# Four conditioned layers on one core: softmax probabilities normalised by POOL before the transposes, instead of the attention outputs by VectorE after the values product

## What is computed

```python
# layer 0: 16 heads of 32, 4 key/value heads, causal in blocks of 128
h = layernorm(x) * (1 + scale) + shift
q, k = rope(h @ Wq.T), rope((h @ Wkd.T) @ Wku.T);  v = (h @ Wkd.T) @ Wvu.T
x = x + softmax(q @ k.T / sqrt(32) + mask) @ v @ Wo.T
# layer 1: 8 heads of 64, one key/value head, then a gated MLP of 2048
q, k, v = rope(h @ Wq.T), rope(h @ Wk.T), h @ Wv.T
x = x + softmax(q @ k.T / 8) @ v @ Wo.T
x = x + (silu(h2 @ Wg.T) * (h2 @ Wu.T)) @ Wd.T
# layer 2: 16 heads of 32, q and k of unit length, bias, then a gelu MLP of 2048
x = x + gamma1 * (softmax(qn @ kn.T + bias) @ v @ Wproj.T + bproj)
x = x + gamma2 * (gelu(h2 @ Wfc1.T) @ Wfc2.T)
# layer 3: experts, layernorm, silu, projection
```

## Times and profile before

| | us |
|---|---|
| runs of the kernel before (3) | 2496.61, 2500.17, 2505.05; median 2500.17 |
| profiled execution | 2504.14, its span 2502.1 |
| PE, PEld busy | 2361.6 (94%), 1477.7 (59%) |
| DVE, ACT, POOL busy | 1199.7 (48%), 1062.8 (42%), 267.2 (11%) |
| attention of layer 0, 1, 2 in the span | 91 to 476, 476 to 843, 1437 to 2005 |

### The profile page before, as it was taken

How to read it: one execution, slowest core, us unless ns; L and a number is a source line. 1 busy time by engine, 2 the same in 40 slices (tenths; PEclk the granted TensorE clock), 3 DMA queues, 4 the chain that set the end, 5 groups by cost and what they waited for, 6 DMA issues and landing times.

```text
span 2502.1 us, 32257 instructions
## 1 busy us (share of the span) xinstructions
PE 2361.6 (94%) x13000; PEld 1477.7 (59%) x13000; DVE 1199.7 (48%) x2466; ACT 1062.8 (42%) x2407; POOL 267.2 (11%) x222
## 2 busy tenths in 40 slices
PE   6889999999999999999999989999999889999998
PEld 2445555455555687888877544445455568888633
DVE  2465564553446434333443254638367655444332
ACT  2465565543435321111113155638457652222373
POOL 3332021121121000000000010101001110000021
PEclk8899999999999999999999979999999999999999
DMA  9200010000001000000001000000001011000001
GB/s 311 72 17 17 1 34 10 9 5 5 9 10 42 26 1 26 26 26 26 26 7 67 17 1 1 1 1 1 1 1 35 18 51 34 17 17 1 1 18 51
DMA packets 45236, 64.95 MB, mean 26 GB/s; under 512 B 8368, under 2 KB 21952, under 8 KB 45088
## 3 DMA queue, kind: packets, MB, share of 16 engines
q1 hardware_dynamic: 44112, 60.38, 7.5%
q0 software_dynamic: 976, 2.51, 0.3%
HBM read 52.66 MB, written 4.19 MB: 23 GB/s over the span
## 4 chain that ended last, share of the span: by engine, by line
PE 85%; ACT 6%; DVE 6%; issue 1%; POOL 1%; DMA 0%; SPq 0%; POOLq 0%; ACTq 0%; DVEq 0%
PE banks L1026 35%; PE banks L388 22%; PE banks L663 8%; PE banks L655 6%; PE banks L679 5%; DVE sb_Pr L735 2%; ACT sb_Pr L765 2%; PE banks L486 1%; PE banks L261 1%; PE banks L689 1%; PE banks L426 1%; ACT sb_PT L770 1%; PE banks L561 1%; PE banks L569 1%; DVE sb_hN L352 1%; ACT sb_t L299 1%
## 5 line engine op out<-in xcount | busy, mean ns | idle before, releaser
L1026 PE MATMUL banks<-sb_HH,sb_Ws 128*128 128x512 f32 x1536 | 494.8, 396 | 12.7 <-DVE sb_HL L943 7.2
L663 PEld LDWEIGHTS banks<-sb_ident,sb_Pr 128*128 128x128 f32 x2176 | 242.7, 143 | 213.8 <-issue 82.2
L663 PE MATMUL banks<-sb_ident,sb_Pr 128*128 128x128 f32 x2176 | 316.7, 284 | 34.7 <-DVE sb_PT L742 12.1
L1026 PEld LDWEIGHTS banks<-sb_HH,sb_Ws 128*128 128x128 f32 x1536 | 291.9, 190 | 78.4 <-issue 17.6
L1026 PE MATMUL banks<-sb_hidH,sb_Ws 128*128 128x512 f32 x1024 | 332.1, 394 | 0.0
L765 ACT ACTIVATE sb_Pr<-sb_Pr,sb_nmax 128x512 f32<-128x512 f32 (+3 forms) x512 | 321.7, 635 | 22.1 <-DVE sb_nmax L735 22.1
L735 DVE CUSTOM_DVE_ANT_0 sb_Pr<-banks,sb_bias 128x512 f32<-128x512 f32 (+3 forms) x512 | 273.7, 587 | 113.8 <-PE banks L655 108.7
L1026 PE MATMUL banks<-sb_HL,sb_Ws 128*128 128x512 f32 x768 | 301.7, 393 | 0.0
L770 ACT ACTIVATE sb_PT<-banks 128x512 f32<-128x512 f32 (+3 forms) x320 | 154.4, 528 | 326.0 <-PE banks L663 325.3
L388 PE MATMUL banks<-sb_hN,sb_W 128*128 128x512 f32 x576 | 268.3, 610 | 9.5 <-ACT sb_hN L321 6.4
L742 DVE COPY sb_PT<-banks 128x512 f32<-128x512 f32 (+3 forms) x320 | 181.1, 603 | 165.0 <-PE banks L663 164.4
(11 more groups left out here) (128 smaller groups left out, 2558.4 us busy)
## 6 DMA issues: line engine op xcount, KB each, us to landing
sb_staged<-in_L_cond_Wfc SPq DMA_DIRECT2D x16, 512.0 KB, 4.3
sb_wada<-in_L_cond_Wada SPq DMA_DIRECT2D x6, 1024.0 KB, 5.6
sb_x<-in_x SPq DMA_DIRECT2D x4, 1024.0 KB, 9.8
sb_staged<-in_L_cond_Wg SPq DMA_DIRECT2D x8, 512.0 KB, 3.5
sb_staged<-in_L_cond_Wu SPq DMA_DIRECT2D x8, 512.0 KB, 4.5
sb_staged<-in_L_cond_Wd SPq DMA_DIRECT2D x8, 512.0 KB, 3.6
out_x<-sb_x SPq DMA_DIRECT2D x4, 1024.0 KB, 4.5
sb_R<-sb_R SPq DMA_DIRECT2D x60, 64.0 KB, 2.0
```

Source lines behind the costliest of these rows:

```text
L663: mm = e.transpose(bank[:, j * P:(j + 1) * P], k.Pr[:, n % 6, j * P:(j + 1) * P], k.ident[:])
L1026: mm = e.matmul(bank, lhsT, rhs, start=i == 0, stop=i == len(mats) - 1)
```

## The change

The probabilities of each unit are normalised before they are transposed. DVE takes the reciprocals of two units' sums at a time (`recip`, 320 instead of 48 instructions, 2 columns instead of 16 or 8), POOL multiplies each unit's probabilities in place by its reciprocal, a column that is repeated along the row (`divide`, 640 instructions on POOL, as wide as the unit's scores), and `turn` waits for `divide` instead of `exp`. The spreads (PE) and the divisions of the outputs (DVE) are gone; the output projection waits for `out`. In the sequence the reciprocal of units 2 and 3 of quad t stands ahead of the four maxima of quad t+1, and that of units 0 and 1 of quad t+1 stands behind its last exponentials and ahead of the copies of units 2 and 3 of quad t. POOL's multiplications follow each.

```diff
@@ Heads.pe
         elif kind == "turn":
-            for due in after(s.name, b, "exp", u):
+            for due in after(s.name, b, "divide", u):
                 e.wait_ge(*due)
@@
-        else:
-            for due in after(s.name, b, "recip", u):
-                e.wait_ge(*due)
-            bank = s.tab.claim(e, s, b, kind, u, after)
-            for i in range(TT):
-                for hl in range(s.per):
-                    o = s.column(u, i, hl)
-                    mm = e.matmul(bank[hl * s.dv:(hl + 1) * s.dv, i * P:(i + 1) * P],
-                                  k.rsum[:, b % 2, o:o + 1].to_broadcast([P, s.dv]), k.ident[:], start=True, stop=True)
@@ Heads.dve
-        elif kind == "recip":
-            for due in after(s.name, b, "exp", (u + 1) * 2 * s.G - 1):
-                e.wait_ge(*due)
-            o = slice(s.column(u, 0, 0), s.column(u + 1, 0, 0))
+        else:
+            for due in after(s.name, b, "exp", 2 * u + 1):
+                e.wait_ge(*due)
+            c, _, i, hl = s.units[2 * u]
+            o = slice(s.column(c, i, hl), s.column(c, i, hl) + 2)
             ins = e.reciprocal(k.rsum[:, b % 2, o], k.sums[:, b % 2, o])
-        else:
-            for due in after(s.name, b, "out", u):
-                e.wait_ge(*due)
-            for due in after(s.name, b, "spread", u):
-                e.wait_ge(*due)
-            ins = e.tensor_tensor(s.out(b, u), s.out(b, u), s.tab.at[(s.name, b, "spread", u)], ALU.mult)
         ins.then_inc(k.done["dve"], 1)
+
+    def pool(s, k, e, b, kind, u, after):
+        for due in after(s.name, b, "recip", u // 2):
+            e.wait_ge(*due)
+        prob = k.Pr[:, (s.first[b] + u) % 6, 0:s.width(u)]
+        e.tensor_tensor(prob, prob, s.stat(k, k.rsum, b, u).to_broadcast([P, s.width(u)]), ALU.mult)\
+            .then_inc(k.done["pool"], 1)
@@ weave
+    def recip(t, half):
+        for h, b, u in units(t)[2 * half:2 * half + 1]:
+            seq.append((h, b, "dve", "recip", u // 2))
+            seq.extend([(h, b, "pool", "divide", u), (h, b, "pool", "divide", u + 1)])
+
...
         copy(t, 0)
         copy(t, 1)
+        recip(t, 1)
         for i in range(4):
             soft(t + 1, i, "dve", "max")
         soft(t + 1, 0, "act", "exp")
         soft(t + 1, 1, "act", "exp")
         point(m)
-        for h, b, c in spreads:
-            seq.extend([(h, b, "pe", "spread", c), (h, b, "dve", "divide", c)])
-        spreads = []
...
                 if g % 2:
-                    seq.extend([(h, b, "act", "out", g // 2), (h, b, "dve", "recip", g // 2)])
-                    spreads.append((h, b, g // 2))
+                    seq.append((h, b, "act", "out", g // 2))
         point(m)
         turn(t, 2)
         turn(t, 3)
         soft(t + 1, 2, "act", "exp")
         soft(t + 1, 3, "act", "exp")
+        recip(t + 1, 0)
         copy(t, 2)
         copy(t, 3)
@@ conditioned_stack
-        divided = lambda name, b: (lambda c: [(name, b, "divide", c)])
+        valued = lambda name, b: (lambda c: [(name, b, "out", c)])
```

More of the change, by code:

```diff
@@ L663, in pe @@
                 mm = e.transpose(bank[:, j * P:(j + 1) * P], k.Pr[:, n % 6, j * P:(j + 1) * P], k.ident[:])
-        elif kind == "values":
+        else:
             c, ip = divmod(u, 2)
@@ L681, in pe @@
                                   start=j == 0, stop=j == tiles - 1)
-        else:
-            for due in after(s.name, b, "recip", u):
-                e.wait_ge(*due)
-            bank = s.tab.claim(e, s, b, kind, u, after)
-            for i in range(TT):
-                for hl in range(s.per):
-                    o = s.column(u, i, hl)
-                    mm = e.matmul(bank[hl * s.dv:(hl + 1) * s.dv, i * P:(i + 1) * P],
-                                  k.rsum[:, b % 2, o:o + 1].to_broadcast([P, s.dv]), k.ident[:], start=True, stop=True)
         mm.then_inc(k.done["pe"], 1)
     def reader(s, kind, u):
-        return {"scores": (s.released, u), "turn": ("copy", u), "spread": ("divide", u), "values": ("out", u // 2)}[kind]
+        return {"scores": (s.released, u), "turn": ("copy", u), "values": ("out", u // 2)}[kind]
     def copy_waits(s, e, k, b, u, after):
@@ L742, in dve @@
             ins = e.tensor_copy(*s.turned(k, b, u))
-        elif kind == "recip":
-            for due in after(s.name, b, "exp", (u + 1) * 2 * s.G - 1):
+        else:
+            for due in after(s.name, b, "exp", 2 * u + 1):
                 e.wait_ge(*due)
-            o = slice(s.column(u, 0, 0), s.column(u + 1, 0, 0))
+            c, _, i, hl = s.units[2 * u]
+            o = slice(s.column(c, i, hl), s.column(c, i, hl) + 2)
             ins = e.reciprocal(k.rsum[:, b % 2, o], k.sums[:, b % 2, o])
-        else:
-            for due in after(s.name, b, "out", u):
-                e.wait_ge(*due)
-            for due in after(s.name, b, "spread", u):
-                e.wait_ge(*due)
-            ins = e.tensor_tensor(s.out(b, u), s.out(b, u), s.tab.at[(s.name, b, "spread", u)], ALU.mult)
-        ins.then_inc(k.done["dve"], 1)
+        ins.then_inc(k.done["dve"], 1)
+    def pool(s, k, e, b, kind, u, after):
[4 more added lines that the diff above has]
+            .then_inc(k.done["pool"], 1)
     def act(s, k, e, b, kind, u, after):
@@ L910, in weave @@
         point(m)
-    assert not spreads and seen[len(mains)] >= len(closing)
+    assert seen[len(mains)] >= len(closing)
     return seq
@@ L1329, in conditioned_stack @@
         scaled = lambda name, b: (lambda c: [(name, b, "scale", c)])
-        divided = lambda name, b: (lambda c: [(name, b, "divide", c)])
+        valued = lambda name, b: (lambda c: [(name, b, "out", c)])
         def post(n, w, gamma=None, free=None, load=None):
             return SideLinear(f"post{n}", [
-                Group(lambda b, g=g: product(w, g, lambda c: attended(b, c), divided(f"heads{n}", b)), "dve",
+                Group(lambda b, g=g: product(w, g, lambda c: attended(b, c), valued(f"heads{n}", b)), "dve",
                       residual_put(g, gamma), load=load, free=free and (lambda b, g=g: free(b, g))) for g in range(C)])
```

## The result

The changed kernel takes 2606.2 us (median of 4 runs, 2603.9 to 2619.2) against 2502.3 for the kernel before: a ratio of 1.043, 95% interval [1.039, 1.047]. Its profiled execution took 2604.7, with a span of 2602.6. It is slower, as forecast, by 104 us where 39 were expected, and it lies outside the range (2470 to 2600).

A forecast was written before the change was run, and what follows sets the result against it. TensorE's in-order queue was taken to bound the kernel. From 2504.1 us, 89 of lateness behind POOL less 50 for removed spreads gave 2543, less 4 to the median 2539; range 2470 to 2600.

The forecast's parts named there:

- What bounds it (TensorE's queue): All three attention stretches: TensorE sets the time, busy 2361.6 of 2502.1 us, with only some 78 us idle there.
- Removal, 50 us: TensorE's queue: 48 spreads take 47 us, up to 22 of waits go too; 50 of 47 to 69 taken.
- POOL's price, 1.23 us: POOL's 640 multiplications: 1.23 us for 512 columns, scaled with width, as its adds and products start 1.23 apart.
- case 3: POOL: repeated-column multiplication cheaper, 0.85 us for 512 columns; lateness 41, gain 67, 2474 us; meets gain at 0.92-1.06; chance 0.22.
- The reciprocals' size (0.15 us each): VectorE: 320 reciprocals of 2 columns at 0.15 us, 48 us in all, about equal to the 44 that leave.
- Their place: VectorE's queue: reciprocals wait for exponentials ahead of maxima, or stand behind side work; counting this, lateness is 143 us.
- case 2: VectorE's queue: the reciprocals' places count too, +143 - 50 = +93, so 2593 us; chance 0.21.
- Lateness, 89 us: TensorE waiting for POOL's queue: 89 us, 39 in layer 0, 9 in layer 1, 41 in layer 2.
- The ledger: All 320 pairs: POOL's possible end compared with TensorE's start, new lateness carried on; 89 us in sum.
- the sum itself, 2504.1 + 89 - 50: Whole kernel: profiled time plus POOL's lateness less the removal, 2543 us, less 4 to the median, 2539.
- Direction and chance (slower, 0.68): Whole kernel: slower by more than 7.5 us, chance 0.68; faster 0.22, within 0.10.
- The signs named: Profile: POOL rows near 1.23 us, POOL 65-75% busy in layer 0, TensorE idle for POOL over 60 us around batch ends.

The follow-up runs named there:

- no_norm: The changed kernel without its reciprocals and multiplications, transposes waiting for the exponentials (probabilities not normalised): 2474.4 us, ratio 0.989 to the kernel before.
- before: The kernel before the change, with spreads and divisions: 2502.3 us.
- the ladder: Kernels adding the change's parts in turn: removal 2474.4 us, reciprocals 2501.8, multiplication two columns wide 2531.6, half width 2557.6, full change 2606.2.
- recip_only: no_norm with the 320 small reciprocals kept at their places in VectorE's queue, nothing waiting for them: 2501.8 us, ratio 1.000 to the kernel before.
- recip_late: The changed kernel with the reciprocals of units 2 and 3 behind the next quad's four maxima: 2690.6 us, ratio 1.077 to the kernel before.
- pool_alone: The changed kernel without reciprocals, POOL multiplying at full width by the row's sum after the pair's exponentials: 2609.7 us, ratio 1.043 to the kernel before.
- after: The complete changed kernel: 2606.2 us, ratio 1.043 to the kernel before.

## Why the prediction was wrong, step by step

- **What bounds it (TensorE's queue).** Right: TensorE still carries 78% of the chain that ended last.
- **Removal, 50 us.** The work that left is 49.9 by the table (50.4 in no_norm), so the step of 16 and 8 products by 1.01 and 0.92 us holds. What it yields is less: no_norm is 25 us faster as a median, 29.6 in the profiled span. Its idle time is the same as before's (143.6 and 140.5), so the waits for the spreads' bank moved elsewhere, and it has 35 us more at 1.2 GHz. I gave their part (up to 22) almost no gain, rightly, but had no term for a loss.
- **POOL's price, 1.23 us.** Too high. Two multiplications behind each other at 512 columns take 2.04 us (the timeline row under the ladder), one 1.039 by the rows, so they start 1.00 apart; for 128, 256 and 384 columns it is 0.36, 0.57 and 0.78. POOL's adds and products of two full operands stay at 1.27 to 1.32. So a repeated column is cheaper. The Trainium skill (GPSIMD Engine Reference, Performance versus the Vector engine) gives about 2.6 cycles an element for a two-operand `tensor_tensor` and, for the best case of a loop, 1.8, 769 ns for 512 elements; the measured 1.00 us lies above the latter, and neither figure is for this form. 1.00 lies inside the 0.92 to 1.06 where case 3 was to meet the gain; the kernel is nevertheless 100 us slower, so the condition of case 3 was as good as met and its result was far off.
- **The reciprocals' size (0.15 us each).** Right: 159 ns, 51.0 us in all against 48. **Their place** was weighed as a case of its own (case 2) and left out of the sum. It belonged in: VectorE waits 105.3 us, in 114 pieces, for an exponential ahead of them, recip_only pays 27 us for them, and recip_late shows what a later start does.
- **Lateness, 89 us.** TensorE's idle time grew by 84.7, in the layers by 40.6, 7.7 and 35.4 against 39, 9 and 41. This agreement is in part luck. The ledger stood at 89 for a price of 1.23 and at 41 for 0.85, so in a straight line some 60 for 1.00 (an estimate), without the reciprocals' places; with them it stood at 143 for 1.23. The price was too high, a real wait was left out, and the two errors worked against each other; how nearly they cancelled is not shown.
- **The step that failed: the sum itself, 2504.1 + 89 - 50.** It priced a wait of TensorE at its length and left TensorE's work at its old speed. The trace of before held the term: 121 us at 1.2 GHz beside 140.5 of idle time, and clocks of 0.97 beside 0.99 in the earlier trace rows. The change took the low time to 253 us, and half of the 131 more is 65.6. With that term and nothing else altered the sum is 2543 + 65.6 = 2609; with the measured idle time (4 us less) 2604.3, and the profiled run took 2604.7. That it closes is the table's arithmetic; what the runs add is the term itself, 66 us by the table or 56 by the stricter count, where the prediction had nothing.
- **Cases and range.** Case 2's value, 2593, was nearest, yet for a sum that lacks the clock. The range's upper end, case 2 with 7 us more, had no room for it. Direction and chance (slower, 0.68) held.
- **The signs named.** L689 and L753 are gone; POOL's rows are 1.04, not 1.23; POOL is busy for 58% of layer 0 (253.1 of 433.8), not 65 to 75; TensorE's idle time for POOL at L662 is over 60 (112.3), gathered around the ends of batches in layer 2 but scattered through every batch of layer 0; layer 1 is shorter, and so is its MLP (609.3 to 605.0). Layer 0 is longer by over 50, the sign of case 2, but by 40.6 of idle time and the rest clock.

**Open.** How much low clock a given idle time brings. It isn't their sum alone: no_norm idles as before does and has 35 us more at 1.2 GHz. Its two middle batches of layer 2 take 150.1 us each with a clock of 0.94 and 9 us idle, against 144.4, 1.00 and 6 in before, with less work in them. pool_alone idles less than after and has more low time. Which arrangement of waits matters, no run separates.

## What to carry to other kernels

Where TensorE is the bound, price a wait as its length and half of the time that it adds at 1.2 GHz; here 85 us of added waits brought 131 us of low clock, so each microsecond cost 1.8, and from rung to rung of the ladder 1.4 to 2.0. Read work, idle time and low time apart, for each stage, before the sum is made. An idle engine put between two others costs by its place and by its length: of the 104 us of POOL's step two columns cost 30 and the rest of the width 74, though it was busy for little more than half of the attention stretches; a later start on half of the pairs cost another 84.

## What the runs showed of the hardware

- A kernel with less TensorE work and the same idle time can run at a lower mean clock: no_norm 0.969 (0.968 to 0.969 in its three runs), before 0.976 (0.976 to 0.982 in the eleven on the same chip).
- POOL's product with a repeated column starts every 0.15 us for 2 columns and every 1.00 for 512, against some 1.23 for two full operands.
- Useless transposes in the waits of after made it 13 us shorter in the profiled execution, though they added 135 us of TensorE work; in the kernel before they made it 39 us longer.
- With POOL busy for 832 us instead of 267, the records of VectorE and ScalarE kept their length (687 and 685 ns, 715 and 714).
